# GpSimd multiplies each scanned state by C in one instruction of 128x2048 instead of two of 128x1024

## The chip, the cores and the metric

The kernel runs on one core of one Trainium2 chip. The metric is the device time of one execution in microseconds (us). A core has five engines with a queue of instructions each: TensorE (PE; its weight loads are listed as PEld), VectorE (DVE), ScalarE (ACT), GpSimd (POOL) and SyncE (SP), which issues the transfers here. Engines meet only at semaphores: an instruction waits until a counter has reached a value, and raises another when it is done. Everything queued behind a waiting instruction waits too.

## The reference

All is float32. The middle part, four layers of a selective scan, takes most of the time:

```
h  = einsum('bhid,oi,od->bho', x, weighted_sum, weight)      # 4 batches x 512 tokens x 256
for _ in range(4):                                           # on layernorm(h)
    xn = rmsnorm(x);  x_in, res = split(xn @ W_in)           # 512 inner channels each
    u  = silu(causal_conv4(x_in) + conv_b)
    dt, B, C = split(u @ W_x)                                # rank 64, 16 states, 16 states
    delta = softplus(dt @ W_dt + b_dt)
    state[s] = exp(delta * A[s]) * state[s] + (delta * u) * B[s]     # scan over the 512 tokens
    y  = sum_s state[s] * C[s] + u * D
    x  = (y * silu(res)) @ W_out
h = h + x;  h = h + ffn(layernorm(h))                        # router to 1 of 4 experts, gelu
```

## The kernel before, in words

There are three parts, one after the other: token mixing (to about 200 us), the scan layers (to about 1840 us) and the expert layer. Only the middle one is touched.

The scan part runs 16 steps `k`, one for each layer and batch. A step has 16 states `s`, and a state has four blocks `d` of 128 channels by 512 tokens. I write (s,d) for a place in a step. State number i = 16k+s lives in `hid[i % 6]`, a ring of six buffers of 128x4x512. For each state:

- ACT writes exp(delta*A) into `hid`, four instructions (`decay`, L434), and delta*u*B in the token-major layout into `dub_t`, four instructions (L447). For s = 6, 7, 10 and 12 POOL does the latter (`times_b`, L353).
- PE turns `dub_t` into channel-major blocks (`b_states`, L706, four transposes for each d) in one of two PSUM banks. `b_states` of block n waits for the scan of block n-2, whose bank it takes.
- DVE scans block d (L554) and counts `scanned`.
- POOL multiplies the scanned state by C (`times_c`, L362), in place, in two halves of two blocks each: half 0 waits for the scan of d=1, half 1 for that of d=3. C lies in `c_rep`, two buffers of two states, filled by SP (L306).
- PE adds the product into four PSUM banks (`sum_states`, L717, four transposes for each d). It does so LAG = 2 states later: at place (s,d) of the step PE first does `b_states(s,d)` and then `sum_states(s-2,d)`. So `sum_states` of state 8, block 0, stands at (10,0). It waits for `hc_ready` at d=0 (half 0) and at d=2 (half 1).

Between these, tables say at which (s,d) an engine does a piece of the next steps' other work: `X_AT`, `R_AT`, `SKIP_AT` (the u*D term, L724, at (10,0) for one) and so on. POOL's extra pieces are `times_b(s+3)` behind the products of s = 3, 4, 7 and 9, `root` (L336) behind state 5, and delta*u of the next step (`times_u`, L343) in two halves: behind half 0 of state 6 and behind half 0 of state 7. PE turns that du later (L661, from (9,2) on). `root` and the u part stop with the last steps: k = 14 has no `root` and no L600 work on PE, and k = 15 has no `times_u` either.

The order of every queue is written out by the loops; no planner moves anything.

Of the kernel before, what the change touches and what calls it, by code (L numbers as in the profile page):

```python
# [4 lines left out]
P = 128  # L5
BATCH, SEQ = 4, 512
# [5 lines left out]
INNER, STATE, CONV, RANK = 512, 16, 4, 64  # L12
NI = INNER // P
# [4 lines left out]
GROUP = 2  # L18
NG = STATE // GROUP
HALF = NI // 2  # L20

TAIL_MEAN, TAIL_VAR, HEAD_MEAN, HEAD_VAR, ROUTER = 0, 1, 2, 3, 5
RING = 6
LAG = 2
DUB = 3
POOL_B = (6, 7, 10, 12)
# [3 lines left out]
def build(nc, x_t, ws_t, w_t, w_in, conv_w, conv_b, w_x, w_dt, b_dt, a_log, d_skip, w_out,  # L30
          w_router, w1, b1, wo, bo, gamma, beta, out):
    f32 = mybir.dt.float32
    ALU = mybir.AluOpType
# [8 lines left out]
    with ctx:  # L42
        def sem(name):
            return ctx.enter_context(nc.semaphore(name))
# [174 lines left out]
        with mam:  # L219
# [14 lines left out]
            hid = sb("hid", [P, RING, NI, SEQ])  # L234
# [39 lines left out]
            scanned = sem("scanned")  # L274
            hc_ready = sem("hc_ready")
# [8 lines left out]
            def live(k):  # L284
                return 0 <= k < STEPS

            with nc.Block() as block:
                @block.sync
                def _(sp):
                    def load_x(k):  # L290
                        if k:
                            sp.wait_ge(xn_ready, k)
                        sp.wait_ge(x_stored, 16 * (k + 1))
                        sp.dma_start(xt[:, :, :], x_dram[k]).then_inc(x_loaded, 16)

                    def store_bc(k):
                        sp.wait_ge(dbl_ready, k + 1)
                        sp.dma_start(bc_dram[k], dbl[RANK:, :]).then_inc(bc_stored, 16)

                    def load_c(k, g):  # L300
                        n = NG * k + g
                        if g == 0:
                            sp.wait_ge(bc_stored, 16 * (k + 1))
                        if n >= 2:
                            sp.wait_ge(hc_ready, 2 * GROUP * (n - 1))
                        sp.dma_start(c_rep[:, n % 2, :, :],  # L306
                                     bc_dram[k, STATE + g * GROUP:STATE + (g + 1) * GROUP].partition_broadcast(P))\
                            .then_inc(c_in[n % 2], 16)

                    def store_x(k):  # L310
                        sp.wait_ge(x_out_ready, DC * (k + 1))
                        sp.dma_start(x_dram[k + BATCH], x_out[:, :, :]).then_inc(x_stored, 16)

                    for k in range(-2, STEPS + 2):
                        if live(k - 2):
                            store_x(k - 2)
                        if live(k):
                            load_c(k, 1)
                        if live(k + 2):
                            load_x(k + 2)  # L320
                        for g in range(2, NG):
                            if live(k):
                                load_c(k, g)
                            if g == 3 and live(k + 1):
                                store_bc(k + 1)
                        if live(k + 1):
                            load_c(k + 1, 0)

                @block.gpsimd
                def _(pool):  # L330
                    nc.gpsimd.memset(half_power[:, :], -0.5).then_inc(half_ready, 1)
                    pool.wait_ge(half_ready, 1)

                    def root(k):
                        pool.wait_ge(ss_ready, k + 1)
                        nc.gpsimd.tensor_tensor(norm[:, :], norm[:, :], half_power[:, :], ALU.pow).then_inc(norm_ready, 1)  # L336

                    def times_u(k, half):
                        pool.wait_ge(delta_ready, NI * k + HALF * (half + 1))
                        if k:  # L340
                            pool.wait_ge(dut_done, TC * k)
                        rows = slice(half * HALF, (half + 1) * HALF)
                        nc.gpsimd.tensor_tensor(du[:, rows, :], delta[:, k % 2, rows, :], u[:, k % 2, rows, :],  # L343
                                                ALU.mult).then_inc(du_ready, 1)

                    def times_b(k, s):
                        i = STATE * k + s
                        if s == POOL_B[0]:
                            pool.wait_ge(du_t_ready, TC * (k + 1))
                            pool.wait_ge(b_t_ready, k + 1)  # L350
                        pool.wait_ge(b_ready, NI * (i - DUB + 1))
                        for tc in range(TC):
                            nc.gpsimd.tensor_scalar(dub_t[:, i % DUB, tc, :], du_t[:, k % 2, tc, :],  # L353
                                                    b_t[:, k % 2, tc, s:s + 1], 1.0, ALU.mult, ALU.mult).then_inc(dub_pool, 1)

                    def times_c(k, s, half):
                        n = NG * k + s // GROUP
                        if half == 0 and s % GROUP == 0:
                            pool.wait_ge(c_in[n % 2], 16 * (n // 2 + 1))
                        pool.wait_ge(scanned, NI * (STATE * k + s) + HALF * (half + 1))  # L360
                        part = hid[:, (STATE * k + s) % RING, half * HALF:(half + 1) * HALF, :]
                        nc.gpsimd.tensor_tensor(part, part, c_rep[:, n % 2, s % GROUP, :].unsqueeze(1)  # L362
                                                .broadcast_to([P, HALF, SEQ]), ALU.mult).then_inc(hc_ready, 1)

                    for k in range(-2, STEPS):
                        for s in range(STATE):
                            for half in range(2):
                                if live(k):
                                    times_c(k, s, half)
                                if live(k + 1) and (s, half) == (6, 0):  # L370
                                    times_u(k + 1, 0)
                                if live(k + 1) and (s, half) == (7, 0):
                                    times_u(k + 1, 1)
                                if live(k + 2) and (s, half) == (5, 1):
                                    root(k + 2)
                                if live(k) and half == 1 and s + 3 in POOL_B:
                                    times_b(k, s + 3)

                @block.scalar
                def _(act):  # L380
# [190 lines left out]
                def _(pe):  # L571
# [138 lines left out]
                    def sum_states(k, s, d):  # L710
                        i = STATE * k + s
                        if s == 0 and k:
                            pe.wait_ge(gated, NI * (k - 1) + d + 1)
                        if d % HALF == 0:
                            pe.wait_ge(hc_ready, 2 * i + d // HALF + 1)
                        for c in range(TC):
                            last = nc.tensor.matmul(y_ps[d][:, c * P:(c + 1) * P], hid[:, i % RING, d, c * P:(c + 1) * P],  # L717
                                                    ident[:, :], start=s == 0 and c == 0, stop=s == STATE - 1,
                                                    is_transpose=True, skip_group_check=True)
                        last.then_inc(summed, 1)  # L720
# [20 lines left out]
                    for k in range(-2, STEPS + 2):  # L741
                        for s in range(STATE):
                            for d in range(NI):
# [3 lines left out]
                                if s >= LAG and live(k):  # L747
                                    sum_states(k, s - LAG, d)
                                if s < LAG and live(k - 1):
                                    sum_states(k - 1, STATE - LAG + s, d)  # L750
# [328 lines left out]
```

## Time and profile before

| | us |
|---|---|
| median of 3 runs | 2278.48 (2276.82 to 2280.76) |
| the profiled execution, its own time | 2275.55 |
| its span, first to last instruction | 2273.6 |
| what lies around the span | 1.95 |
| PE busy | 2058.8 (91%) |
| DVE busy | 1577.9 (69%) |
| POOL busy | 1478.5 (65%) |
| ACT busy | 1474.0 (65%) |
| mean granted clock of TensorE | 0.964 of 2.4 GHz |

The shares are means over three parts with different limits; POOL for one does nearly all of its work inside the 1640 us of the scan part. PE's busy time is modelled from pipelined matmuls and overlaps; the weight loads (PEld) show better when PE moves on.

### The profile page before, as it was taken

How to read it: one execution, taken by the hardware profiler on the slowest of the kernel's cores; microseconds unless marked ns; L12 is line 12 of the kernel's file. 1: busy time of each engine (PE TensorE's matmuls, PEld its weight loads, DVE VectorE, ACT ScalarE, POOL GpSimd, SP SyncE). 2: the span in 40 equal slices, each digit the busy share in tenths (PEclk: the TensorE clock that was granted, in tenths of full speed). 3: DMA queues.
4: the chain of work that ended last, by engine and by line, in shares of the span. 5: the costliest groups of instructions: out<-in, count | busy, mean ns of one | idle time of the engine just before them, and what ended most of it. 6: DMA issues, size and time to landing. Idle time of an engine off the chain costs nothing.

```text
span 2273.6 us, 30364 instructions
## 1 busy us (share of the span) xinstructions
PE 2058.8 (91%) x11680; PEld 1427.5 (63%) x11680; DVE 1577.9 (69%) x1552; ACT 1474.0 (65%) x2322; POOL 1478.5 (65%) x835
## 2 busy tenths in 40 slices
PE   7567989999999999999999999999999867999997
PEld 3234767777776777777777767777777733444443
DVE  1326888897988888887979788888888833333411
ACT  0117888888888888978888888888889710111110
POOL 0004989888898979888988879797989930000000
PEclk9768999999999999999999999999999987999998
DMA  5200111111112111111111121111111140000000
GB/s 189 97 29 25 42 48 47 58 51 54 56 39 65 39 65 39 61 44 57 41 65 56 39 66 39 66 39 58 47 48 60 44 163 14 0 28 0 10 10 10
DMA packets 34423, 114.15 MB, mean 50 GB/s; under 512 B 6180, under 2 KB 8868, under 8 KB 33768
## 3 DMA queue, kind: packets, MB, share of 16 engines
q1 hardware_dynamic: 34280, 112.22, 14.2%
q8 instruction: 93, 1.52, 0.3%
q14 instruction: 50, 0.41, 0.1%
HBM read 96.47 MB, written 15.73 MB: 49 GB/s over the span
## 4 chain that ended last, share of the span: by engine, by line
PE 49%; DVE 15%; ACT 14%; issue 11%; POOL 6%; DMA 0%; POOLq 0%; DVEq 0%; SPq 0%; ACTq 0%
PE b_ps L706 10%; PE y_ps L717 8%; PE work_ps L1023 7%; DVE hid L554 7%; ACT hid L434 6%; ACT dub_t L447 5%; POOL hid L362 5%; DVE u L523 4%; PE bank_b L600 3%; PE bank_a L615 3%; PE bank_b L615 2%; PE bank_a L624 2%; PE out_ps L1041 2%; PE bank_b L649 1%; PE bank_a L649 1%
## 5 line engine op out<-in xcount | busy, mean ns | idle before, releaser
L554 DVE TENSOR_TENSOR_SCAN hid<-hid,b_ps 128x512 f32<-128x512 f32 x1024 | 1213.3, 1210 | 245.8 <-PE b_ps L706 225.1
L362 POOL TENSOR_TENSOR hid<-hid,c_rep 128x1024 f32<-128x1024 f32 x512 | 1203.2, 2370 | 201.7 <-DVE hid L554 201.5
L706 PEld LDWEIGHTS b_ps<-ident,dub_t 128*128 128x128 f32 x4096 | 481.4, 143 | 377.3 <-issue 215.4
L706 PE MATMUL b_ps<-ident,dub_t 128*128 128x128 f32 x4096 | 637.2, 279 | 58.3 <-DVE hid L554 52.4
L434 ACT ACTIVATE hid<-delta,neg_a 128x512 f32<-128x512 f32 x1024 | 653.0, 711 | 0.4
L717 PE MATMUL y_ps<-ident,hid 128*128 128x128 f32 x4096 | 620.6, 275 | 10.8 <-POOL hid L362 10.7
L447 ACT ACTIVATE dub_t<-du_t,b_t 128x512 f32<-128x512 f32 x768 | 490.4, 712 | 45.5 <-PE b_ps L706 43.7
L717 PEld LDWEIGHTS y_ps<-ident,hid 128*128 128x128 f32 x4096 | 483.9, 143 | 16.3 <-POOL hid L362 15.2
L1023 PE MATMUL work_ps<-zm,w_sb 128*128 128x512 f32 x512 | 226.5, 596 | 0.0
L893 ACT ACTIVATE inter<-work_ps 128x512 f32<-128x512 f32 x32 | 19.1, 597 | 287.4 <-PE work_ps L1023 287.4
L875 POOL TENSOR_TENSOR fsq<-y 128x1024 f32<-128x1024 f32 x4 | 7.6, 1892 | 276.6 <-DVE y L917 276.6
L1023 PEld LDWEIGHTS work_ps<-zm,w_sb 128*128 128x128 f32 x512 | 98.2, 192 | 123.8 <-issue 123.8
L353 POOL TENSOR_SCALAR dub_t<-du_t,b_t 128x512 f32<-128x512 f32 x256 | 172.6, 695 | 0.0
L600 PE MATMUL bank_b<-xn,w_in_sb 128*128 128x512 f32 x256 | 139.6, 635 | 18.5 <-DVE u L523 15.9
L523 DVE SCALAR_TENSOR_TENSOR u<-bank_b,conv_w_sb,u 128x511 f32<-128x511 f32 (+2 forms) x192 | 139.6, 727 | 0.8
L691 PE MATMUL bank_a<-y_d,w_out_sb 128*128 128x512 f32 x256 | 130.3, 595 | 1.4 <-ACT y_d L419 0.7
L415 ACT ACTIVATE du_t<-bank_a 128x512 f32<-128x512 f32 x64 | 37.9, 592 | 72.4 <-PE bank_a L661 72.4
L343 POOL TENSOR_TENSOR du<-delta,u 128x1024 f32<-128x1024 f32 x32 | 75.5, 2361 | 11.5 <-ACT delta L410 11.5
L615 PE MATMUL bank_a<-w_in_sb,xn 128*128 128x512 f32 x128 | 67.2, 609 | 15.8 <-DVE hid L554 14.1
L875 POOL TENSOR_TENSOR fsq<-z 128x1024 f32<-128x1024 f32 x4 | 7.6, 1892 | 113.0 <-DVE z L917 113.0
L962 DVE SCALAR_TENSOR_TENSOR y<-out_ps,fvec,z 128x512 f32<-128x512 f32 x8 | 5.6, 746 | 95.8 <-PE out_ps L1041 95.8
L154 PE MATMUL tok_ps<-xT,wc 128*128 128x512 f32 x128 | 58.2, 612 | 14.7 <-DMA xT<-x_t 14.7
(112 smaller groups left out, 1639.5 us busy)
## 6 DMA issues: line engine op xcount, KB each, us to landing
c_rep<-bc_dram SPq DMA_DIRECT2D x128, 512.0 KB, 3.6
xT<-x_t SPq DMA_DIRECT2D x4, 2048.0 KB, 8.5
xt<-x_dram SPq DMA_DIRECT2D x16, 512.0 KB, 3.8
x_dram<-x_out SPq DMA_DIRECT2D x16, 512.0 KB, 2.9
w_sb<-L_ffn_W SPq DMA_DIRECT2D x4, 1024.0 KB
h_dram<-h SPq DMA_DIRECT2D x4, 512.0 KB, 2.8
x_dram<-xo SPq DMA_DIRECT2D x4, 512.0 KB, 2.6
hb<-h_dram SPq DMA_DIRECT2D x4, 512.0 KB, 5.2
```

The lines of the kernel that those rows point to most:

```text
L353: nc.gpsimd.tensor_scalar(dub_t[:, i % DUB, tc, :], du_t[:, k % 2, tc, :], b_t[:, k % 2, tc, s:s + 1], 1.0, ALU.mult, ALU.mult).then_inc(d ...
L362: nc.gpsimd.tensor_tensor(part, part, c_rep[:, n % 2, s % GROUP, :].unsqueeze(1) .broadcast_to([P, HALF, SEQ]), ALU.mult).then_inc(hc_read ...
L434: nc.scalar.activation(hid[:, i % RING, d, :], delta[:, k % 2, d, :], ACT.Exp, scale=neg_a[:, d, s:s + 1]).then_inc(decay_ready, 1)
L447: nc.scalar.activation(dub_t[:, i % DUB, tc, :], du_t[:, k % 2, tc, :], ACT.Copy, scale=b_t[:, k % 2, tc, s:s + 1]).then_inc(dub_act, 1)
L523: nc.vector.scalar_tensor_tensor(u[:, k % 2, m, t:], bank_b[:, 0:SEQ - t], conv_w_sb[:, m, w:w + 1], u[:, k % 2, m, t:], ALU.mult, ALU.add ...
L554: nc.vector.tensor_tensor_scan(hid[:, i % RING, d, :], hid[:, i % RING, d, :], b_ps[d % 2][:, :], 0.0, ALU.mult, ALU.add)\
L600: ins = nc.tensor.matmul(bank_b[:, :], w_in_sb[:, c, m * P:(m + 1) * P], xn[:, c, :], start=c == 0, stop=c == DC - 1)
L615: ins = nc.tensor.matmul((bank_a if tc % 2 == 0 else bank_b)[:, :], xn[:, c, tc * P:(tc + 1) * P], w_in_sb[:, c, INNER:], start=c == 0, st ...
L691: ins = nc.tensor.matmul(bank_a[:, :], w_out_sb[:, d, m * P:(m + 1) * P], y_d[:, d, :], start=d == 0, stop=d == NI - 1)
L706: last = nc.tensor.transpose(b_ps[d % 2][:, c * P:(c + 1) * P], dub_t[:, i % DUB, c, d * P:(d + 1) * P], ident[:, :])
L717: last = nc.tensor.matmul(y_ps[d][:, c * P:(c + 1) * P], hid[:, i % RING, d, c * P:(c + 1) * P], ident[:, :], start=s == 0 and c == 0, sto ...
L1023: last = nc.tensor.matmul(work_ps[c % 4][:, :], w1_sb[:, m, e, cols], zm[:, b % 2, e, m, :], start=False, stop=e == EXPERTS - 1 and m == D ...
```

## The change

The loop over halves in POOL's program is gone. `times_c` handles all four blocks of a state in one instruction and waits for the scan of d=3. `hc_ready` counts states, so that SP waits for GROUP*(n-1) and PE's `sum_states` waits once for each state, at d=0. The two halves of `times_u` now stand behind the whole product of state 6 and of state 7.

```diff
                         if n >= 2:
-                            sp.wait_ge(hc_ready, 2 * GROUP * (n - 1))
+                            sp.wait_ge(hc_ready, GROUP * (n - 1))
...
-                    def times_c(k, s, half):
+                    def times_c(k, s):
                         n = NG * k + s // GROUP
-                        if half == 0 and s % GROUP == 0:
+                        if s % GROUP == 0:
                             pool.wait_ge(c_in[n % 2], 16 * (n // 2 + 1))
-                        pool.wait_ge(scanned, NI * (STATE * k + s) + HALF * (half + 1))
-                        part = hid[:, (STATE * k + s) % RING, half * HALF:(half + 1) * HALF, :]
+                        pool.wait_ge(scanned, NI * (STATE * k + s + 1))
+                        part = hid[:, (STATE * k + s) % RING, :, :]
                         nc.gpsimd.tensor_tensor(part, part, c_rep[:, n % 2, s % GROUP, :].unsqueeze(1)
-                                                .broadcast_to([P, HALF, SEQ]), ALU.mult).then_inc(hc_ready, 1)
+                                                .broadcast_to([P, NI, SEQ]), ALU.mult).then_inc(hc_ready, 1)
...
-                            for half in range(2):
-                                if live(k):
-                                    times_c(k, s, half)
-                                if live(k + 1) and (s, half) == (6, 0):
-                                    times_u(k + 1, 0)
-                                if live(k + 1) and (s, half) == (7, 0):
-                                    times_u(k + 1, 1)
-                                if live(k + 2) and (s, half) == (5, 1):
-                                    root(k + 2)
-                                if live(k) and half == 1 and s + 3 in POOL_B:
-                                    times_b(k, s + 3)
+                            if live(k):
+                                times_c(k, s)
+                            if live(k + 1) and s in (6, 7):
+                                times_u(k + 1, s - 6)
+                            if live(k + 2) and s == 5:
+                                root(k + 2)
+                            if live(k) and s + 3 in POOL_B:
+                                times_b(k, s + 3)
...
-                        if d % HALF == 0:
-                            pe.wait_ge(hc_ready, 2 * i + d // HALF + 1)
+                        if d == 0:
+                            pe.wait_ge(hc_ready, i + 1)
```

POOL's queue in the middle of a step, from `root` behind state 5 on, before (L362 is a product with C, L343 delta*u, L353 the product with B):

```order
L336 TENSOR_TENSOR norm<-norm,half_power 128x4 [waits ss_ready]
L362 TENSOR_TENSOR hid<-hid,c_rep 128x1024 [waits scanned,c_in1]
L343 TENSOR_TENSOR du<-delta,u 128x1024 [waits dut_done,delta_ready]
L362 TENSOR_TENSOR hid<-hid,c_rep 128x1024 [waits scanned] x2
L343 TENSOR_TENSOR du<-delta,u 128x1024 [waits dut_done,delta_ready]
L362 TENSOR_TENSOR hid<-hid,c_rep 128x1024 [waits scanned]
L353 TENSOR_SCALAR dub_t<-du_t,b_t 128x512 [waits b_ready]
```

and the same stretch now:

```order
L336 TENSOR_TENSOR norm<-norm,half_power 128x4 [waits ss_ready]
L362 TENSOR_TENSOR hid<-hid,c_rep 128x2048 [waits scanned,c_in1]
L343 TENSOR_TENSOR du<-delta,u 128x1024 [waits dut_done,delta_ready]
L362 TENSOR_TENSOR hid<-hid,c_rep 128x2048 [waits scanned]
L343 TENSOR_TENSOR du<-delta,u 128x1024 [waits dut_done,delta_ready]
L353 TENSOR_SCALAR dub_t<-du_t,b_t 128x512 [waits b_ready]
```

The second delta*u has moved behind the whole product of state 7; the product with B that follows (for state 10) has the same work ahead of it as before.

PE's queue around place (10,0), before; the first L717 with a wait is `sum_states` of state 8, block 0, the second is block 2:

```order
L706 MATMUL b_ps<-ident,dub_t 128x128 [waits scanned,dub_pool]
L706 MATMUL b_ps<-ident,dub_t 128x128 x3
L717 MATMUL y_ps<-ident,hid 128x128 [waits hc_ready]
L717 MATMUL y_ps<-ident,hid 128x128 x3
L724 MATMUL y_ps<-diag_skip,u 128x128 x4
L706 MATMUL b_ps<-ident,dub_t 128x128 [waits scanned]
...
L717 MATMUL y_ps<-ident,hid 128x128 [waits hc_ready]
```

and now (the new program is three lines shorter above this point, so L706 reads L703, L717 reads L714 and L724 reads L721):

```order
L703 MATMUL b_ps<-ident,dub_t 128x128 [waits scanned,dub_pool]
L703 MATMUL b_ps<-ident,dub_t 128x128 x3
L714 MATMUL y_ps<-ident,hid 128x128 [waits hc_ready]
L714 MATMUL y_ps<-ident,hid 128x128 x3
L721 MATMUL y_ps<-diag_skip,u 128x128 x4
L703 MATMUL b_ps<-ident,dub_t 128x128 [waits scanned]
...
L714 MATMUL y_ps<-ident,hid 128x128 x4
```

No PE instruction has moved; the wait at block 2 is gone, and the wait at block 0 is for all four blocks.

## Rows read from the trace of the kernel before

**Rows 1.** Costliest groups: line, engine, out<-in, shape, count | busy, mean ns | idle before.

```profile
L362 POOL TENSOR_TENSOR hid<-hid,c_rep 128x1024 f32<-128x1024 f32 x512 | 1203.2, 2370 | 201.7 <-DVE hid L554 201.5
```

**Rows 2.** Busy us by stretch: steps k=7, 8, 14 and 15; PEclk, DMA share, GB/s.

```profile
921.60:1029.11 107.51, 102.52 (x669) 78.97 (x668) 88.56 (x89) 88.35 (x142) 91.49 (x52) 0.95 0.15 50
1029.11:1132.10 102.99, 98.07 (x669) 75.94 (x668) 88.45 (x88) 88.10 (x142) 91.26 (x52) 1.00 0.15 53
1651.62:1746.70 95.08, 88.95 (x632) 70.98 (x631) 77.98 (x72) 83.88 (x136) 87.60 (x50) 1.00 0.15 51
1746.70:1838.60 91.90, 82.00 (x609) 68.43 (x607) 77.38 (x72) 64.22 (x105) 89.54 (x50) 0.98 0.15 53
```

**Rows 3.** Waits: engine, line <- what it waited for: us, times, longest.

```profile
POOL hid L362 <- DVE hid L554: 201.5, 183, 25.5
...
PEld y_ps L717 <- POOL hid L362: 15.2, 19, 1.9
```

**Rows 4.** Timeline, k=7: second half-product of state 12, then PE's sum of it.

```profile
1009.64 2.37 POOL L362 TENSOR_TENSOR hid<-hid,c_rep 128x1024 f32<-128x1024 f32 x1 [0.43 <-DVE hid L554]
...
1015.03 0.47 PEld L717 LDWEIGHTS y_ps<-ident,hid 128*128 128x128 f32 x4
```

**Rows 5.** Timeline of POOL, k=8, from half 1 of state 3 on.

```profile
1055.01 2.36 POOL L362 TENSOR_TENSOR hid<-hid,c_rep 128x1024 f32<-128x1024 f32 x1 [1.11 <-DVE hid L554]
1057.36 2.68 POOL L353 TENSOR_SCALAR dub_t<-du_t,b_t 128x512 f32<-128x512 f32 x4
1060.02 4.70 POOL L362 TENSOR_TENSOR hid<-hid,c_rep 128x1024 f32<-128x1024 f32 x2
...
1071.99 1.01 POOL L336 TENSOR_TENSOR norm<-norm,half_power 128x4 f32<-128x4 f32 x1
...
1075.31 2.35 POOL L343 TENSOR_TENSOR du<-delta,u 128x1024 f32<-128x1024 f32 x1
...
1086.93 2.68 POOL L353 TENSOR_SCALAR dub_t<-du_t,b_t 128x512 f32<-128x512 f32 x4
1089.59 9.35 POOL L362 TENSOR_TENSOR hid<-hid,c_rep 128x1024 f32<-128x1024 f32 x4
```

**Rows 6.** Timeline of PE's weight loads, k=8, places (9,0) to (11,0).

```profile
1086.10 0.47 PEld L717 LDWEIGHTS y_ps<-ident,hid 128*128 128x128 f32 x4
...
1092.01 0.42 PEld L717 LDWEIGHTS y_ps<-ident,hid 128*128 128x128 f32 x4 [0.22 <-POOL hid L362]
1092.40 0.97 PEld L724 LDWEIGHTS y_ps<-diag_skip,u 128*128 128x128 f32 x8
1093.29 0.47 PEld L706 LDWEIGHTS b_ps<-ident,dub_t 128*128 128x128 f32 x4
...
1098.42 0.42 PEld L706 LDWEIGHTS b_ps<-ident,dub_t 128*128 128x128 f32 x4 [0.97 <-issue]
```

**Rows 7.** Timeline of DVE, k=8: scan (10,1), then the next three.

```profile
1095.32 1.22 DVE L554 TENSOR_TENSOR_SCAN hid<-hid,b_ps 128x512 f32<-128x512 f32 x1
...
1097.09 3.44 DVE L554 TENSOR_TENSOR_SCAN hid<-hid,b_ps 128x512 f32<-128x512 f32 x3
```

**Rows 8.** Timeline of PE's weight loads, k=15, around a wait for POOL.

```profile
1780.86 0.42 PEld L706 LDWEIGHTS b_ps<-ident,dub_t 128*128 128x128 f32 x4 [0.85 <-POOL dub_t L353]
1783.19 0.42 PEld L717 LDWEIGHTS y_ps<-ident,hid 128*128 128x128 f32 x4 [1.91 <-POOL hid L362]
...
1784.93 0.87 PEld L706 LDWEIGHTS b_ps<-ident,dub_t 128*128 128x128 f32 x4
```

**Rows 9.** Busy us of the stretch behind it, and PEclk.

```profile
1783.90:1787.30 3.40, 3.40 (x19) 3.40 (x18) 2.22 (x2) 3.00 (x5) 3.40 (x2) 0.51 0.18 59
```

**Rows 10.** POOL's groups by form, among them the smallest of 128x4.

```profile
L336 POOL TENSOR_TENSOR norm<-norm,half_power 128x4 f32<-128x4 f32 x16 | 16.3, 1020 | 54.5 <-DVE norm L504 54.5
L875 POOL TENSOR_TENSOR fsq<-y 128x1024 f32<-128x1024 f32 x4 | 7.6, 1892 | 276.6 <-DVE y L917 276.6
...
L331 POOL MEMSET half_power<- 128x4 f32 x1 | 0.1, 102 | 107.3 <-POOLq L102 107.3
```

**Rows 11.** Timeline at the end of the scan part, k=15.

```profile
1836.10 1.29 DVE L536 TENSOR_TENSOR yg_t<-y_ps,gate_t 128x512 f32<-128x512 f32 x2 [3.05 <-PE y_ps L717]
1837.32 1.09 PE L717 MATMUL y_ps<-ident,hid 128*128 128x128 f32 x8 [0.81 <-POOL hid L362]
```

## The prediction, written before the changed kernel ran

> **What bounds the kernel now.** I first read the busy time by stretch [rows 2]. A full step takes 102.99 us. POOL, which looks idle for a third of the span, is busy for 91.26 us of it, more than DVE (88.45) and ACT (88.10); in k=14 and 15 it is busy for 87.60 of 95.08 and 89.54 of 91.90 us. Then the waits [rows 3]: POOL waits for DVE 183 times and 201.5 us in all, PE's sums wait for POOL only 19 times and 15.2 us. So POOL idles in one part of a step and has no air in another. The timeline shows the two parts. In the quiet part (states 11 to 3) POOL waits for each scan. In the dense part, from state 3 on, its four products with B, the root and the two delta*u are queued among the products with C, and it runs without a gap: from 1055.01 every row begins where the one before ended [rows 5]. It is caught by PE at one place: the sum of state 8 at (10,0) waits for the half that ends at about 1091.95 [rows 6]. This row stands for eleven: of the steps k = 0 to 13 only the three with a fall of the clock (k = 3, 7, 10) give POOL some 2 us more there. What is left of a step is the loop of PE (L706), DVE (L554) and PE again, which neither engine leads alone.
>
> **The change, part by part.**
>
> *The instruction.* Back to back, four half-products fill 9.34 us (1089.59 to the next row at 1098.93) [rows 5]: 2.335 each, 4.67 for a state. The 1024 elements run at the same pace in a longer instruction; what one instruction fewer saves is a fixed part that the trace doesn't show apart. Bounds: nothing, or nearly all of the 1.02 us that the smallest TENSOR_TENSOR takes (4 elements, but a power, which may be slow by itself), while the smallest MEMSET takes 0.102 [rows 10]. I take the MEMSET, less the 0.035 us by which neighbours overlap (2.37 long, 2.335 apart) [rows 1, 5]: 0.07 saved, 4.60 for a state. Were it only this, 16 x 0.07 = 1.1 us of POOL time would go in each step.
>
> The Trainium skill (GPSIMD Engine Reference, Elementwise — side-by-side cycle accounting) has 4497 ns for a tensor_tensor of 2048 fp32 elements and puts its time down to the elements, with a dispatch of tens of cycles. By that figure a state would cost 4.50 and the stall below would be 0.6 us shorter; the trace's own 1892 and 2370 ns for 1024 elements [rows 10, 1] show that the pace depends on what else runs, so I stay with the rows.
>
> *The quiet part.* The product now starts with the scan of d=3 and ends 4.60 us later, not 2.3. State 12 of k=7: the scan of d=3 is done at 1009.64, the whole product would end at 1014.3, and PE wants it at 1015.03 [rows 4]. The rows stand for a pattern: the quiet states have 0.7 to 2.6 us to spare in this way. Nothing is late; cost 0. SP's loads of C wait for the same ends of products as before, and the other buffer covers two states: 0.
>
> *The dense part.* Here the lost head start counts. Half 0 of state 3 used to be done while DVE still scanned blocks 2 and 3. Now the product starts at 1055.01 with all its work ahead. The queue behind it, by the rows (product 4.60, with B 2.66, root 0.99, delta*u 2.32): state 3 to 1059.6, B to 1062.3, state 4 to 1066.9, B to 1069.5, state 5 to 1074.1, root to 1075.1, state 6 to 1079.7, delta*u to 1082.0, state 7 to 1086.65, delta*u to 1089.0, B to 1091.6, state 8 to 1096.2. What PE wants: state 7 at 1086.10 (0.55 late), and state 8 at 1092.01, or 4.2 us late. It used to be released after half of state 8 (2.335) and with 2.335 of state 3 done early; 4.67 - 6 x 0.07 is the same 4.2. The moved delta*u is done at 1089.0, and PE turns it only at about 1090.
>
> *What of the 4.2 us reaches the end.* Queued behind the sum of state 8 on PE are the u*D term and `b_states(10,1)`, 1.28 us later [rows 6]. DVE still has scans, a tap and scan (10,0) to do and asks for (10,1) only at 1095.32 [rows 7]. Now that block is turned from 1097.5 and ready at about 1098.3, so DVE is 3.0 us late. PE is 4.2 late at first, but has 0.97 us of idle before (11,0) [rows 6], where it falls back to the same 3.1. I take 3.1 us a step; bounds 2 and 4.2. State 10 is then done at 1108.1, where PE wants it at 1104.9 + 3.1: no second stall. The quiet part sets the queue back, and the same happens in the next step. The steps with this are k = 0 to 13: 14 x 3.1 = 43.4 us.
>
> *The clock.* PE stands still from about 1092.5 to 1096.2, 3.7 us. In k=15 it stood for 0.85 and 1.91 us with one block between [rows 8], and then ran a stretch of 3.4 us at a granted clock of 0.51, the 1.2 GHz level [rows 9]: four loads took 0.87 us instead of 0.47 [rows 8, 6]. There half of 3.4 us was lost to PE; with PE's loads filling three quarters of a step [rows 2], that is 1.3 us on the loop. A stall twice as long as that one should bring it in most steps: 14 x 1.3 = 18.2 us. Bounds: 0, and 4.5 (107.51 - 102.99 [rows 2], a step whose clock was low for about 10 us near (6,0)). Those long falls came in 3 steps of 16; with other step lengths they may come in none or in six, +-13 us, which I keep for the range.
>
> The Trainium skill (TensorE: Matmul & The Clock Gate, Why this matters for your kernels) warns of idle gaps between bursts of matmuls, after which the engine falls back to the lower clock. It speaks against this change, which makes such a gap; by it the fall comes in every step, and the sum stays 2345.
>
> *k = 14 and 15.* Here POOL sets the pace to the end [rows 2]. It starts 2.33 us later behind state 3 of k=14, saves 29 x 0.07 = 2.0, and where products follow each other, the way back (product done, sum 0.44, turn 0.8, three scans of 1.13) takes about 4.8 against a product's 4.6: some 15 states at 0.1 are 1.5. At the end the sums and gatings of d=0 and 1, which were over before the last half [rows 11], come behind it: 1.2. With a fall of the clock or two: 5 us, bounds 0 and 12.
>
> **Sum.** 2275.55 + 43.4 + 18.2 + 5 = 2342.15 for an execution like the profiled one, which lies 2.93 below the median: 2345 us.
>
> **The rivals.**
> 1. The stall is there, the clock holds: 2278.5 + 43.4 + 5 = 2327. For it: PE also idles 0.97 us elsewhere at full clock; against: rows 8 and 9.
> 2. The falls are long, 4.5 us each: 2278.5 + 43.4 + 63 + 5 = 2390. For it: k=7. Against: that fall came where PE had small matmuls (16 and 64 rows), and behind (10,0) it has full ones.
> 3. The loop swallows most of the lateness, because PE catches up behind the stall over several states: about 1 us a step, 2278.5 + 14 + 5 = 2298. Against: the idle of PE in rows 6 is all that I found beside waits for DVE.
> 4. Faster: the fixed part of a TENSOR_TENSOR is what the power shows, 0.98 us. A state then costs 3.69, the queue waits for scans again at states 6 and 7, state 8 is done at 1093.7, 1.7 late, of which 1.1 are taken up: 14 x 0.6 = 8 us lost, and k = 14 and 15 gain up to 29 x 0.98 less what DVE and PE need, some 20: 2278 + 8 - 20 = 2266. It decides from about 0.7 us saved an instruction. Against: the MEMSET.
>
> **How the numbers follow.** Forecast 0.38, rival 1 0.22, rival 2 0.22, rival 3 0.12, rival 4 0.06. Rivals 3 and 4 hold the little that could be no change. From the cases: faster by over 0.2% 0.05, within 0.2% 0.03, slower 0.92 (0.2% is about what a measurement of this kernel tells from no change). The range reaches from rival 3 to rival 2: 2303 to 2392.
>
> **What the new profile would show.** The product with C at about 4.6 us (3.7 would speak for rival 4). POOL's wait for DVE a little up in the quiet part, and no waits of PE for POOL there. At (10,0) of k = 0 to 13 a wait of the weight load of some 3 to 4 us for POOL, and one of about 0.3 or none at other places. A step of 106 to 108 us. PEclk below 1 just behind each such wait, for rows of some 3 us (rival 2: 10 us; rival 1: none). I am wrong if a step is still near 103 us, or if the product is slower for each element in the long form.

## The result, and the profile after

The changed kernel takes 2383.57 us (median of 4 runs, 2380.30 to 2388.18) against 2278.40: slower by 4.6%, ratio 1.0462 (95% interval 1.0438 to 1.0486). That is the way forecast (2345) and inside the range (2303 to 2392), but with 105 us of loss where I had summed 66.6. The profiled execution took 2380.35 us, span 2378.3, mean granted clock 0.937.

The costliest group of POOL, from the page of the changed kernel:

```profile
L362 POOL TENSOR_TENSOR hid<-hid,c_rep 128x2048 f32<-128x2048 f32 x256 | 1163.6, 4549 | 350.1 <-DVE hid L551 350.1
```

Against [rows 1] POOL does the same products in 40 us less, and its idle time has grown by 148 us. The waits of the changed kernel, as in [rows 3]:

```profile
POOL hid L362 <- DVE hid L551: 350.1, 177, 30.8
DVE hid L551 <- PE b_ps L703: 319.9, 385, 6.1
...
PEld y_ps L714 <- POOL hid L362: 78.0, 38, 4.0
```

PE's loads used to wait 15.2 us for POOL and now wait 78.0. DVE waits for PE 319.9 us, where the kernel before had:

```profile
DVE hid L554 <- PE b_ps L706: 225.1, 333, 2.7
```

POOL's dense part in step k=8, as in [rows 5]:

```profile
1107.03 4.55 POOL L362 TENSOR_TENSOR hid<-hid,c_rep 128x2048 f32<-128x2048 f32 x1 [3.52 <-DVE hid L551]
...
1125.90 1.01 POOL L336 TENSOR_TENSOR norm<-norm,half_power 128x4 f32<-128x4 f32 x1
1127.16 4.53 POOL L362 TENSOR_TENSOR hid<-hid,c_rep 128x2048 f32<-128x2048 f32 x1 [0.26 <-DVE hid L551]
...
1143.51 9.01 POOL L362 TENSOR_TENSOR hid<-hid,c_rep 128x2048 f32<-128x2048 f32 x2
```

State 3 starts with the scan of its d=3 and state 8 starts 36.5 us later, as the sum of the rows said. One row was not foreseen: state 6 waits for its own scan too. PE's weight loads around (10,0), as in [rows 6]:

```profile
1143.76 0.47 PEld L703 LDWEIGHTS b_ps<-ident,dub_t 128*128 128x128 f32 x4
1148.09 0.72 PEld L714 LDWEIGHTS y_ps<-ident,hid 128*128 128x128 f32 x4 [3.85 <-POOL hid L362]
1148.79 1.83 PEld L721 LDWEIGHTS y_ps<-diag_skip,u 128*128 128x128 f32 x8
1150.49 0.87 PEld L703 LDWEIGHTS b_ps<-ident,dub_t 128*128 128x128 f32 x4
...
1154.40 0.97 PEld L721 LDWEIGHTS y_ps<-diag_skip,u 128*128 128x128 f32 x8
```

and DVE's scan (10,1), as in [rows 7]:

```profile
1151.87 1.22 DVE L551 TENSOR_TENSOR_SCAN hid<-hid,b_ps 128x512 f32<-128x512 f32 x1 [4.02 <-PE b_ps L703]
```

The loads stand for 3.85 us (the stall), and behind them eight loads take 1.83 us instead of 0.97: the clock has fallen. I call a stretch at the 1.2 GHz level a fall, short up to 6.8 us and long from 10 us on. The stretches of the changed kernel, columns as in [rows 2]: the steps k=1, 7 and 8, k=14, then k=15 with the end of the scan part.

```profile
309.41:416.67 107.26, 98.17 (x664) 76.47 (x663) 88.64 (x89) 86.76 (x139) 88.89 (x36) 0.98 0.14 46
968.08:1081.13 113.05, 105.62 (x669) 82.25 (x668) 88.95 (x89) 88.32 (x142) 88.93 (x36) 0.92 0.14 48
1081.13:1189.89 108.76, 100.80 (x669) 78.80 (x668) 88.73 (x88) 88.09 (x142) 88.92 (x36) 0.97 0.14 50
1746.64:1846.30 99.66, 90.54 (x631) 72.28 (x630) 78.11 (x72) 83.93 (x136) 87.40 (x34) 0.98 0.15 49
1846.30:1942.40 96.10, 81.92 (x594) 68.48 (x593) 75.82 (x69) 64.32 (x105) 87.59 (x33) 0.96 0.14 50
```

From k=3 on, steps of 113.05 and 108.8 us alternate. Two shorter stretches say why, one from k=9 near (6,0), one from k=8 behind (10,0):

```profile
1229.30:1243.00 13.70, 13.70 (x49) 9.84 (x48) 5.83 (x8) 8.27 (x12) 8.88 (x5) 0.51 0.12 38
...
1147.40:1154.20 6.80, 6.11 (x30) 6.11 (x31) 2.31 (x3) 0.69 (x2) 6.80 (x5) 0.51 0.09 22
```

Every step from k = 0 to 14 has a short fall behind the stall (3.4 or 6.8 us), and k = 3, 5, 7, 9, 11 and 13 have a long one of 13.7 us as well. Of the short falls in k = 0 to 13, six are 6.8 us long (k = 0, 4, 6, 8, 10, 12) and eight are 3.4 us. PE is busy all through the long one (13.70 of 13.70 us), so that no wait of PE lies in it.

### The profile page after: what moved, and what is told of

Its sections match the earlier page's. It is cut to its first block, busy times and chain, and to the rows that moved or that the text cites. A ratio compares the mean times of both kernels' runs of the same rounds, so it can differ in the third digit from the quotient of the medians.

```text
span 2378.3 us, 30093 instructions
## 1 busy us (share of the span) xinstructions
PE 2115.8 (89%) x11680; PEld 1479.5 (62%) x11680; DVE 1582.9 (67%) x1552; ACT 1474.6 (62%) x2322; POOL 1440.4 (61%) x579
## 3 DMA queue, kind: packets, MB, share of 16 engines
q1 hardware_dynamic: 34280, 112.22, 13.7%
## 4 chain that ended last, share of the span: by engine, by line
PE 49%; POOL 13%; ACT 12%; DVE 12%; issue 9%; DMA 0%; POOLq 0%; DVEq 0%; SPq 0%; ACTq 0%
PE b_ps L703 10%; POOL hid L362 9%; PE y_ps L714 9%; PE work_ps L1020 7%; DVE hid L551 5%; ACT hid L431 5%; ACT dub_t L444 5%; PE bank_b L597 2%; POOL dub_t L353 2%; DVE u L520 2%; PE bank_b L612 2%; PE bank_a L612 2%; PE bank_a L621 2%; PE out_ps L1038 2%; PE y_ps L721 2%
## 5 line engine op out<-in xcount | busy, mean ns | idle before, releaser
L551 DVE TENSOR_TENSOR_SCAN hid<-hid,b_ps 128x512 f32<-128x512 f32 x1024 | 1216.0, 1210 | 341.3 <-PE b_ps L703 319.9
L362 POOL TENSOR_TENSOR hid<-hid,c_rep 128x2048 f32<-128x2048 f32 x256 | 1163.6, 4549 | 350.1 <-DVE hid L551 350.1
L703 PEld LDWEIGHTS b_ps<-ident,dub_t 128*128 128x128 f32 x4096 | 500.2, 146 | 363.0 <-issue 211.9
L714 PE MATMUL y_ps<-ident,hid 128*128 128x128 f32 x4096 | 640.3, 281 | 69.3 <-POOL hid L362 69.1
L703 PE MATMUL b_ps<-ident,dub_t 128*128 128x128 f32 x4096 | 654.0, 284 | 46.7 <-DVE hid L551 41.8
L714 PEld LDWEIGHTS y_ps<-ident,hid 128*128 128x128 f32 x4096 | 499.3, 146 | 79.6 <-POOL hid L362 78.0
L353 POOL TENSOR_SCALAR dub_t<-du_t,b_t 128x512 f32<-128x512 f32 x256 | 172.7, 697 | 0.0
L343 POOL TENSOR_TENSOR du<-delta,u 128x1024 f32<-128x1024 f32 x32 | 75.9, 2371 | 4.5 <-ACT delta L407 4.5
L721 PE MATMUL y_ps<-diag_skip,u 128*128 128x128 f32 x512 | 77.3, 301 | 0.0
```

What stands on the lines that cost most here:

```text
L551: nc.vector.tensor_tensor_scan(hid[:, i % RING, d, :], hid[:, i % RING, d, :], b_ps[d % 2][:, :], 0.0, ALU.mult, ALU.add)\
L703: last = nc.tensor.transpose(b_ps[d % 2][:, c * P:(c + 1) * P], dub_t[:, i % DUB, c, d * P:(d + 1) * P], ident[:, :])
```

## The experiments

"Step" is the time from scan (0,0) of one step to that of the next, read where the clock granted in the step is 1.00 if there is such a step.

**The clock apart from the stall.** The changed kernel with `FILL = 20` useless transposes on PE inside the stall of k = 0 to 13:

```diff
                                     b_states(k, s, d)
+                                if live(k) and live(k + 2) and at == (10, 0):
+                                    pe.wait_ge(scanned, NI * (STATE * k + s))
+                                    for c in range(FILL):
+                                        nc.tensor.transpose(b_ps[1][:, c % TC * P:(c % TC + 1) * P], ident[:, :], ident[:, :])
```

> The changed kernel with 20 more transposes of the identity into the bank that is about to be overwritten, on PE behind b_states(10,0) in the steps k=0 to 13: 2.8 us of work inside the stall of 3.8 us, so that it delays nothing and TensorE isn't idle. Clock theory: the stall itself costs 3.1 us a step, the fall of the clock behind it 1.2 to 2.7 us, and the second, longer fall near (6,0) in every second step comes only where the step length brings it. With the first fall gone 2325 to 2350 us, PEclk 1 behind (10,0). Rival, the whole of the loss is the stall and the clock costs nothing on the path: 2375 to 2390.

Measured 2326.33 us (2325.84 to 2338.47), ratio 1.0219 (1.0192 to 1.0247). PE's weight loads in k=8, and below them the step's busy times:

```profile
1125.54 2.17 PEld L748 LDWEIGHTS b_ps<-ident 128*128 128x128 f32 x20 [1.26 <-DVE hid L552]
1128.17 0.42 PEld L715 LDWEIGHTS y_ps<-ident,hid 128*128 128x128 f32 x4 [0.47 <-POOL hid L363]
1128.56 0.97 PEld L722 LDWEIGHTS y_ps<-diag_skip,u 128*128 128x128 f32 x8
```

```profile
1061.17:1167.12 105.95, 100.35 (x689) 78.12 (x688) 88.64 (x89) 88.10 (x142) 88.95 (x36) 1.00 0.16 51
```

More work on PE makes the kernel 57 us faster. PE is done with it 0.47 us before POOL's product is ready, so that it delays nothing. The eight loads are back at 0.97 us and the step is 105.95 us: the stall alone costs 105.95 - 102.99 = 2.96 us. What a step of the changed kernel takes beyond 105.95 us is clock. In this profile, its slowest run, four steps still had a long fall near (6,0).

**The two halves of the change, each alone.** In the kernel before, first the late start:

```diff
-                        pool.wait_ge(scanned, NI * (STATE * k + s) + HALF * (half + 1))
+                        pool.wait_ge(scanned, NI * (STATE * k + s + 1))
```

> The kernel before with one part of the change alone: both half-products wait for the scan of d=3 (late start); two instructions, PE still waits half by half. Queue theory: the chain from state 3 to the first half of state 8 starts 2.33 us later, the sum of state 8 is 2.1 us late on PE, about 1.1 of it are taken up behind it: 1.0 to 1.5 us for each of 14 steps, some 3 us at the end, 2293 to 2305 us, if the clock holds; with a fall of the clock in every step up to 2330. Rival, that the price hangs on the late release alone: 2279 to 2284.

2311.13 us, ratio 1.0138 (1.0121 to 1.0155). PE waits 0.66 us for the product with B of state 10 and 1.90 us for state 8, and every step from k = 0 to 13 has a fall of 3.4 us there (weight loads of k=8, then the step):

```profile
1110.96 0.42 PEld L706 LDWEIGHTS b_ps<-ident,dub_t 128*128 128x128 f32 x4 [0.66 <-POOL dub_t L353]
1113.28 0.56 PEld L717 LDWEIGHTS y_ps<-ident,hid 128*128 128x128 f32 x4 [1.90 <-POOL hid L362]
1113.82 1.83 PEld L724 LDWEIGHTS y_ps<-diag_skip,u 128*128 128x128 f32 x8
```

```profile
1048.06:1153.88 105.82, 99.59 (x669) 77.59 (x668) 88.64 (x88) 88.08 (x142) 91.16 (x52) 0.98 0.15 51
```

The same with the stall filled (the edit above with 8 transposes):

> The kernel with the late start alone and two instructions, and 8 transposes of the identity on PE in front of the sum at (10,0), 1.1 us inside its stall of 1.9 us. Clock theory: the fall of 3.4 us behind the stall goes, and a step of 105.83 us comes down by 1.2 to 1.6 us to some 104.4: 2290 to 2300 us if no long falls come. Rival (the 2.8 us a step are the late product itself): 105.8 us a step still, 2305 to 2315.

2310.98 us, ratio 1.0136 (1.0120 to 1.0151), so as a whole no gain; but the steps read as expected, 104.18 us without a fall:

```profile
1152.30:1256.48 104.18, 99.23 (x677) 76.80 (x676) 88.53 (x89) 88.09 (x142) 91.11 (x52) 1.00 0.16 52
```

What the short falls gave back, five long falls near (6,0), of 4.1 to 5.8 us each, took again. The forecast of the total failed by that condition.

Late release:

```diff
-                        if d % HALF == 0:
-                            pe.wait_ge(hc_ready, 2 * i + d // HALF + 1)
+                        if d == 0:
+                            pe.wait_ge(hc_ready, 2 * i + 2)
```

> The kernel before with the other part alone: PE's sums wait at d=0 for both half-products of the state (late release); start, order and instructions as before. Queue theory: the second half of state 8 ends 2.33 us after the first, so the sum is 2.1 us late on PE, and states 7 and 10 0.9 and 1.4: the same 2293 to 2305 us, up to 2330 with falls of the clock. Rival, that the price hangs on the late start alone: 2279 to 2284.

2315.77 us (2307.97 to 2330.08), ratio 1.0167 (1.0126 to 1.0209); the median is above the 2305 of a clock that holds. The profiled execution is the slowest of the four, and nine of its steps have a long fall. In four others (k = 1, 5, 10 and 12) a wait of 0.88 us at state 7 and a stall of 1.69 us at state 8 bring no fall behind them, and the step is 104.19 us (weight loads and busy times of k=10):

```profile
1343.46 0.42 PEld L717 LDWEIGHTS y_ps<-ident,hid 128*128 128x128 f32 x4 [1.69 <-POOL hid L362]
```

```profile
1278.23:1382.42 104.19, 98.13 (x669) 75.94 (x668) 88.64 (x89) 88.11 (x141) 91.41 (x52) 1.00 0.15 52
```

So each part costs 1.2 us a step, 2.33 less the 1.1 that the loop takes up, and neither rival (one part alone carries it) holds. Together they cost 2.96, more than the sum of 2.4, which fits the 1.1 being there only once.

**The instruction count alone.** The changed kernel with two half-products, both waiting for d=3, and PE for both:

> The changed kernel with its product cut in two instructions again; both wait for the scan of d=3, PE waits for both, delta*u stands behind the second. What differs from the changed kernel is the count of instructions alone. The changed kernel's product takes 4.55 us and would take 4.67 here in sum: six of them before the sum of state 8 make the stall some 0.8 to 1.0 us longer, 2390 to 2400 us. If the one long instruction saved nothing on the path, 2380 to 2385.

2374.05 us, ratio 1.0412 (1.0393 to 1.0431). This is a miss: it is faster than the changed kernel, not slower. Step 8, with a fall of 6.8 us as in the changed kernel's step 8:

```profile
1075.96:1185.19 109.23, 100.75 (x669) 78.67 (x668) 88.73 (x88) 88.11 (x142) 91.14 (x52) 0.97 0.15 50
```

Like against like, 109.23 against 108.76, the long instruction does save 0.47 us a step; PE waits 0.85 and 4.02 us at states 7 and 8 here, and 0.44 and 3.85 in the changed kernel. But all steps of this kernel from k=2 to 13 are 109.2 us and have no long fall, while the changed kernel has one in every second step.

**PE asks later.** LAG = 3 in both kernels, with the gating at (2,0) to (2,3), the second half of the R pieces at (3,0) to (3,3), and two u*D pieces at (7,0) and (7,3):

> The changed kernel with PE's sum of a state three states behind its turn instead of two (LAG 3); the gating of the step before, the last R pieces and the first two u*D pieces stand one to five states later so that nothing waits in a circle. PE asks for state 8 some 6 us later than before, at (11,0). Theory (the loss is PE waiting at the sum of state 8): the stall and the falls behind it go; with the shorter POOL time of k=14 and 15 2270 to 2300 us. Rival (the long instruction slows the engines beside it, or the late product costs elsewhere, as by the ring of six states): above 2330.

> The kernel before with the same LAG 3 and the same moved pieces: the base for the run above. Theory: within 1% of it, either way; it takes away 0.2 us of waiting at (10,0) in 11 steps and adds what the moved pieces cost: 2265 to 2295 us. If the changed kernel's long product helps when nobody waits for it, this one is some 2 to 5 us slower than the run above, from k=14 and 15.

2356.34 us (ratio 1.0332, 1.0312 to 1.0352) and 2355.19 us (1.0333, 1.0318 to 1.0349). Both totals miss: the moved pieces made a wait of their own at (3,0) (PE for ACT's gate, up to 3.3 us, and a fall behind it), the same in both. The pair still answers the question. From k = 1 to 13 PE waits for POOL no more in either, and step 8 of whole and of halves is the same:

```profile
1065.56:1174.74 109.18, 101.37 (x669) 77.55 (x668) 88.82 (x89) 88.22 (x142) 88.82 (x36) 0.97 0.14 50
```

```profile
1073.77:1182.94 109.17, 101.36 (x669) 77.55 (x668) 88.82 (x88) 88.20 (x142) 91.42 (x52) 0.97 0.14 50
```

Both steps hold a fall of 6.8 us, and steps of 109.2 us also came from another kernel, so an equal length could hide a difference. The stretch of the same steps from scan (6,0) to the end has no fall in it, and is the same too, whole first:

```profile
1109.24:1174.74 65.50, 62.44 (x430) 48.40 (x428) 56.94 (x58) 54.26 (x88) 57.67 (x24) 1.00 0.11 41
```

```profile
1117.46:1182.94 65.48, 62.41 (x429) 48.39 (x428) 56.92 (x57) 54.23 (x88) 59.52 (x33) 1.00 0.13 41
```

Where nobody waits for it, the whole product costs nothing, and gives nothing: POOL's 2.6 us less work are idle time. In k = 14 and 15, where POOL has no air, somebody does wait: PE stands for the products with B, 7.7 us against 6.6, and each of the two steps is 1.3 us longer with whole products (99.3 against 98.1 in k=14).

**Which states carry it.** `WHOLE` lists states with a whole product in k = 0 to 13, the rest as before:

```diff
+                        if s in WHOLE and k < STEPS - 2:
+                            if half == 0:
+                                pool.wait_ge(scanned, NI * (STATE * k + s + 1))
+                                ... (one product of all four blocks, which raises hc_ready by 2)
+                            return
```

> Whole products of 128x2048 for twelve of sixteen states (all but 3, 7, 8 and 10), k = 0 to 13; halves for those four and in k = 14 and 15; delta*u behind the whole of state 6 and behind half 0 of state 7 as before. Queue theory: only the early start of state 3 and the early release of 7, 8 and 10 count, the other twelve cost nothing: a step of 102.9 to 103.1 us, 2275 to 2281 us. Rival, each whole product costs a little of the loop wherever it stands: 12/16 of the 3.0 us a step, 2305 or more.

2332.34 us, ratio 1.0231 (1.0193 to 1.0268), step 105.04 without a fall (k=3). The expectation was wrong, and so was what my working says of state 6. POOL's rows in this kernel's k=2, first the product of state 6, then that of state 8:

```profile
459.61 4.53 POOL L365 TENSOR_TENSOR hid<-hid,c_rep 128x2048 f32<-128x2048 f32 x1 [1.69 <-DVE hid L562]
...
476.12 4.70 POOL L370 TENSOR_TENSOR hid<-hid,c_rep 128x1024 f32<-128x1024 f32 x2
```

POOL, in time again at state 6, stands 1.69 us for its scan of d=3. Before, half 0 went ahead and delta*u filled the time to the scan. PE waits 1.9 us for state 8 in k=2 as in k=3, but only k=2 has a fall (3.4 us) behind the wait; the two steps:

```profile
413.55:519.17 105.62, 99.61 (x669) 77.61 (x668) 88.83 (x88) 88.12 (x142) 89.66 (x40) 0.98 0.16 51
```

```profile
519.17:624.21 105.04, 98.17 (x669) 75.94 (x668) 88.63 (x88) 88.10 (x142) 89.66 (x40) 1.00 0.15 52
```

> As the run with twelve whole states, but state 6 in halves too, so that eleven are whole (all but 3, 6, 7, 8, 10). In that run the whole product of state 6 waited for the scan of d=3 (it began 2.2 us later in the step than half 0 had), and the sum of state 8 was 2.1 us late again. Corrected queue theory: the dense part has two places where the early start counts, state 3 and state 6; with both, and the early release of 7, 8 and 10, the step is 102.9 to 103.1 us where the clock doesn't fall, 2275 to 2283 us. Rival, whole products cost the loop by themselves: a step over 104.5 us still.

2314.17 us, ratio 1.0165 (1.0144 to 1.0187); step 103.50 without a fall (k = 2, 3, 9, 11, 12), with eleven of sixteen states whole. The loss of a step is down from 2.05 to 0.5 us, not to nothing. State 4 waits 0.70 us for its scan in the same way, and at (10,0) PE waits 0.73 us; but at (11,0) it waits once more, 0.53 us, for the whole product of state 9, which halves would have released earlier. (POOL at state 4 of k=2, PE's two waits, then the step.)

```profile
445.75 4.57 POOL L365 TENSOR_TENSOR hid<-hid,c_rep 128x2048 f32<-128x2048 f32 x1 [0.70 <-DVE hid L562]
...
477.52 0.42 PEld L725 LDWEIGHTS y_ps<-ident,hid 128*128 128x128 f32 x4 [0.73 <-POOL hid L370]
...
484.37 0.42 PEld L725 LDWEIGHTS y_ps<-ident,hid 128*128 128x128 f32 x4 [0.53 <-POOL hid L365]
```

```profile
414.11:517.61 103.50, 98.15 (x669) 75.93 (x668) 88.55 (x89) 88.11 (x142) 89.47 (x41) 1.00 0.16 52
```

Eight of its steps had a long fall, which is most of the 35 us above the kernel before.

**Versions meant to beat both.** Whole products for states 4, 5 and 11 only:

> A version meant to beat both: the kernel before, with whole products of 128x2048 only for states 4, 5 and 11 (k = 0 to 13), where POOL starts late for want of time and PE asks 2 us or more after the end; all others in halves. Each saves 0.15 to 0.17 us on POOL's queue; two of them stand before state 8, where PE waits 0.2 us now: at most 0.2 to 0.3 us for each of 11 steps, 2275 to 2279 us; a change under 0.2% would not be told from none.

2278.54 us, ratio 0.9997 (0.9987 to 1.0006): no difference. This run also says which wait the 0.5 us above are. State 4 waits for its scan and PE waits at (10,0) as there, but nobody waits for state 9, and the step is that of the kernel before (POOL and PE in k=8, then the step):

```profile
1067.32 4.57 POOL L365 TENSOR_TENSOR hid<-hid,c_rep 128x2048 f32<-128x2048 f32 x1 [0.71 <-DVE hid L562]
...
1099.04 0.42 PEld L725 LDWEIGHTS y_ps<-ident,hid 128*128 128x128 f32 x4 [0.70 <-POOL hid L370]
```

```profile
1035.67:1138.65 102.98, 97.92 (x669) 75.97 (x668) 88.44 (x88) 88.08 (x142) 90.88 (x49) 1.00 0.16 53
```

So a wait of 0.7 us at (10,0) is taken up, and the rest in the run with eleven states goes with the late release of state 9. No run had state 9 alone in halves.

Then the product with B of state 10 on ACT, under either kernel:

```diff
-POOL_B = (6, 7, 10, 12)
+POOL_B = (6, 7, 12)
```

> The changed kernel with the product with B of state 10 on ACT instead of POOL (POOL_B = 6, 7, 12): 2.67 us less in POOL's queue before the sum of state 8, 2.55 us more on ACT. Queue theory: the stall of 3.8 us shrinks to 1.2 to 1.5 us, of which the loop takes up some 1.1; no fall behind it: a step of 103.0 to 103.5 us if ACT's 90.6 of 103 us hide it, 2275 to 2300 us with long falls by chance. Rival, ACT becomes the bound between states 8 and 11: 105 us or more a step, over 2310.

> The kernel before with the same move, the base for the run above and a version that may beat both: no wait of 0.2 us at state 8, and POOL, which sets the pace in k = 14 and 15, has 5.3 us less to do there: 2268 to 2278 us. Rival as above, ACT as the bound: 2285 or more.

The runs gave 2296.29 us with whole products, ratio 1.0111 (1.0048 to 1.0174), and the step without a fall is 103.40 us instead of 105.95: taking 2.67 us out of the queue takes 2.55 us out of the loss. With halves 2274.66 us, ratio 0.9985 (0.9976 to 0.9995): the one version ahead of both, by less than 0.2%. A full step stays as it was; k=14 and 15 are shorter than in [rows 2]:

```profile
926.23:1029.21 102.98, 97.92 (x669) 75.94 (x668) 88.43 (x88) 90.31 (x146) 88.84 (x48) 1.00 0.16 53
1656.19:1748.72 92.53, 88.89 (x632) 71.03 (x631) 77.96 (x73) 85.82 (x139) 85.04 (x46) 1.00 0.16 53
```

## Why the prediction was right, and where its sum fell short

The way, the place and the stall were right. The sum was not: the loss was 104.8 us where 66.6 were added up, and 2383.57 us lies nearer to rival 2's 2390 than to my 2345. Rival 2 came close by luck, since it had 4.5 us of clock behind every stall; the falls there cost 26.6/14 = 1.9 us on average, and the rest came from another place. The difference of the two profiled executions is 2380.35 - 2275.55 = 104.8 us. Term by term, forecast and measured:

| term | forecast | measured | from |
|---|---|---|---|
| the stall at (10,0), k = 0 to 13 | 43.4 | 41.4 | 14 x 2.96, run with the stall filled |
| the short fall behind it | 18.2 | 26.6 | what is left of those 14 steps |
| long falls near (6,0), against before | 0 | 23.3 | 6 x 6.16 - 3 x 4.54, states 6 and 7 of those steps |
| k = 14 and 15 | 5 | 9.3 | 4.6 and 4.7, scan to scan |
| before the first step, and the rest | 0 | 4.2 | scan part, behind code that did not change, begins 3.7 us later |

- *Quiet part:* right. PE waits for no product there, with the margins of [rows 4]; the pair with LAG 3 shows that a late product costs nothing where nobody waits for it. POOL's wait for DVE, though, went up by 148 us and not "a little".
- *The instruction:* 4.549 us where I had 4.60 to the next one, that is 4.635 long. Two halves take 9.34/2 = 4.67 back to back [rows 5], one whole about 4.50 (two fill 8.99, from 1143.51 to the next row at 1152.50). The saving is 0.17 us, not 0.07, nearer to the smallest MEMSET's whole 0.102 than to the 1.02 of the power. Rival 4 is out. The 4497 ns that the Trainium skill gives (GPSIMD Engine Reference, Elementwise — side-by-side cycle accounting) were closer than my choice.
- *The dense part:* the lateness was right (4.2 forecast; loads stand 3.85, and 0.44 more at state 7), the pass-through too (3.1 against 2.96). The chain was not: I let it run from state 3 without a stop, and state 6 came out 0.1 us behind its scan by my numbers. With the true 4.50 POOL is ahead there and waits. State 6's early start counts beside state 3's: with it the step went from 105.04 to 103.50 us in the two runs with `WHOLE`. What state 3's is worth by itself no run shows.
- *The clock:* the mechanism was right, the size was not. I took falls of 3.4 us at 1.3 us. Eight of the fourteen are that long, and cost 1.3 us in k=1 (107.26 against 105.95) and 1.6 in k=2; the six others are 6.8 us, and the step with one is 108.76 against 105.95, 2.8 us. What decides between the two lengths is open. Rival 1 is out; rival 2 named the length wrongly for this place.
- *What the sum lacked:* the long falls. I kept them out of it as chance, with +-13 us for none or six, and they are the larger part of the shortfall (23.3 of 38 us). They came in six steps, the bound I had named, but at 6.16 us each instead of 4.5. A longer stall does not bring more of them: the run with two instructions has a longer stall, no long fall in k = 1 to 13, and takes 9.5 us less. That the length of the step does is a guess, which no run tests.
- *k = 14 and 15:* 9.3 inside the bounds of 0 to 12. The rows of 99.66 and 95.08 show that POOL's busy time did not grow (87.40 against 87.60), so POOL's extra time is idle time; that it is the way back from a whole product to the next start is my reading. The terms of that part do not add up either: 0.44 + 0.8 + 3 x 1.13 are 4.63, not 4.8, and 4.8 against 4.6 would be 0.2 a state, not 0.1. Both steps had falls, and how much is clock was not taken apart; the pair with LAG 3 gives 1.3 us a step at equal falls in k=14.
- *The range:* its lower end, 2303, leaves out rival 3's own 2298, to which it was said to reach. The result does not hang on it.

What stays open: why the long falls are 13.7 us here and 10.2 before, and what brings them. No run set the length of a step by itself. Nor is it known when a short fall follows a wait: with twelve whole states the same 1.9 us brought one in k = 0 to 2 and none in k=3.

## What to carry to other kernels

An instruction that is merged waits for its last input and releases with its last output, and pays at both ends wherever its queue has no slack. Ask at each place who waits, not how busy the engine is. Look for it also in the middle of a dense stretch: an early half may be what fills the time until the next input. And where TensorE is led into waiting, count the clock behind the wait as a term of its own; here it was larger than the wait.

## What the runs showed of the hardware

- Idle PE can cost twice. A wait of 3.6 to 3.9 us brought 3.4 to 6.8 us at a granted clock near 0.5. One of 0.66 and then 1.90 us brought 3.4 us in k = 0 to 13 of the late start, 0.41 and then 1.9 us brought it in some steps of the run with twelve whole states and not in others, and 0.88 and then 1.69 us brought none in four steps of the late release. Twenty needless transposes inside the wait brought the kernel from 2383.6 to 2326.3 us.
- Different kernels fell into the same step lengths: 109.2 us with whole and half products at LAG 3 and with two instructions, 105.8 us in thirteen steps running of the late start. In the changed kernel the pair of steps is 113.05 + 108.8 = 221.9 us, and its low stretches come back in the same places of each pair. The run-to-run spread of the kernels with long falls (2307.97 to 2330.08 for the late release) is larger than that of the kernel before (2276 to 2283), so a difference of some 10 us between them need not come from their instructions.
- A GpSimd product of 128x2048 takes 4.549 us and two of 128x1024 4.67 us back to back: 0.12 to 0.17 us is all that merging two into one saves.
